# Down product of three of ten row tiles from row-scaled fp16 weight halves, residual added at evacuation

## The reference, cut to what matters

```python
def _ste_round(v):
    return v + jax.lax.stop_gradient(jnp.round(v) - v)
def _act_fake_quant(x, clip_factor):
    scale = sigmoid(clip_factor) * jnp.max(jnp.abs(x)) / QMAX      # one number for the whole tensor
    return jnp.clip(_ste_round(x / scale), -QMAX - 1.0, QMAX) * scale
def _weight_fake_quant(w):
    scale = jnp.max(jnp.abs(w), axis=1, keepdims=True) / QMAX      # one number for each output row
    return jnp.clip(_ste_round(w / scale), -QMAX - 1.0, QMAX) * scale
def ffn(x, clip_x, clip_down, w_gate, w_up, w_down):
    xq = _act_fake_quant(x, clip_x[0])
    gate = jnp.einsum('bsh,ih->bsi', xq, _weight_fake_quant(w_gate))
    up = jnp.einsum('bsh,ih->bsi', xq, _weight_fake_quant(w_up))
    h = _act_fake_quant(jax.nn.silu(gate) * up, clip_down[0])
    return jnp.einsum('bsi,hi->bsh', h, _weight_fake_quant(w_down))
xn = _layernorm(x)
x = x + gcn(xn, edges) + linear_attention(xn)
x = x + ffn(_layernorm(x))
return x
```

## Time and profile before

| what | value |
|---|---|
| median of 3 runs | 743.32 us |
| the profiled execution's own time | 743.04 us |
| its span, first to last instruction | 740.9 us |
| what lies around the span | 2.14 us |
| PE, DVE, POOL, ACT busy | 712.0, 495.0, 272.1, 208.8 us |
| down stage, first matmul to the end | 716.38 to 740.9 us |

### The profile page before, as it was taken

One profiled execution on the slowest core, in us unless ns is written; L12 is line 12 of the kernel. 1 busy time (PEld: TensorE's weight loads), 2 busy tenths in 40 slices (PEclk: granted clock), 3 DMA queues, 4 the chain that ended last, 5 costly groups with the idle time before them and its releaser, 6 DMA issues.

```text
span 740.9 us, 12159 instructions
## 1 busy us (share of the span) xinstructions
PE 712.0 (96%) x3843; PEld 365.9 (49%) x3843; DVE 495.0 (67%) x978; ACT 208.8 (28%) x346; POOL 272.1 (37%) x403
## 2 busy tenths in 40 slices
PE   4999999999999999999999999999999999999993
PEld 2455555555555554566544444444444444445751
DVE  7878887887666656556932213567777778766767
ACT  5133334553333244446212213420000000012440
POOL 4576767898666646540010000011111111110018
PEclk9999999999999999999999999999999999999997
DMA  9752422551000000003030110052222232100506
GB/s 342 216 140 59 108 42 72 171 171 58 0 0 0 0 2 1 2 0 114 1 114 0 67 46 0 23 174 65 57 72 54 61 85 64 33 12 1 114 13 264
DMA packets 52765, 52.20 MB, mean 70 GB/s; under 512 B 36482, under 2 KB 37514, under 8 KB 52720
## 3 DMA queue, kind: packets, MB, share of 16 engines
q1 hardware_dynamic: 52720, 51.61, 23.3%
HBM read 37.96 MB, written 5.12 MB: 58 GB/s over the span
## 4 chain that ended last, share of the span: by engine, by line
PE 69%; issue 12%; DVE 10%; POOL 4%; ACT 2%; DMA 2%; DVEq 1%; POOLq 0%; SPq 0%; ACTq 0%
PE bank L537 31%; PE bank L730 13%; PE bank L703 10%; PE bank L611 10%; POOL mem L496 2%; DVE mem L1032 2%; PE bank L522 2%; ACT mem L830 2%; PE bank L554 2%; DVE counts L1122 2%; DVE mem L1202 1%; DMA mem<-in_x 1%; PE bank L678 1%; DVE mem L1048 1%; DMA mem<-in_L_gnn_W 1%
## 5 line engine op out<-in xcount | busy, mean ns | idle before, releaser
L537 PE MATMUL bank<-mem 128*128 128x512 f16 x1440 | 327.6, 381 | 4.9 <-DVE mem L1048 1.7
L537 PEld LDWEIGHTS bank<-mem 128*128 (+1 forms) x1440 | 137.9, 98 | 158.6 <-issue 7.0
L448 POOL TENSOR_SCALAR hot_src<-iota_p,src_col 125x128 bf16<-125x128 bf16 x252 | 174.5, 707 | 14.1 <-issue 14.1
L1122 DVE TENSOR_TENSOR counts<-bank,counts 128x120 f32 x328 | 92.4, 282 | 49.2 <-issue 8.5
L611 PE MATMUL bank<-mem 128*128 128x512 f16 (+2 forms) x576 | 105.2, 339 | 0.8 <-DVE mem L1161 0.8
L730 PE MATMUL bank<-mem 128*128 128x512 f16 (+1 forms) x504 | 105.5, 369 | 0.0
L703 PE MATMUL bank<-mem 128*128 128x512 f16 x400 | 88.0, 379 | 0.0
L611 PEld LDWEIGHTS bank<-mem 128*128 128x128 f16 (+1 forms) x576 | 55.2, 98 | 42.4 <-DVE mem L1161 1.4
L730 PEld LDWEIGHTS bank<-mem 128*128 128x128 f16 x504 | 49.3, 98 | 53.7
L850 ACT ACTIVATE src_gap<-iota_p,loT 125x128 bf16<-125x128 bf16 x84 | 33.5, 399 | 115.5 <-PE bank L522 106.9
L485 POOL TENSOR_TENSOR mem<-mem 128x1024 f32<-128x1024 f32 x10 | 23.5, 2350 | 113.3 <-DMA mem<-in_L_mix_bo 113.3
(11 more groups left out here) (150 smaller groups left out, 645.7 us busy)
## 6 DMA issues: line engine op xcount, KB each, us to landing
mem<-in_x SPq DMA_DIRECT2D x18, 512.0 KB, 3.9
out_x<-mem SPq DMA_DIRECT2D x9, 512.0 KB
mem<-in_L_mix_Wk SPq DMA_DIRECT2D x4, 1024.0 KB, 9.4
mem<-in_L_mix_Wv SPq DMA_DIRECT2D x4, 1024.0 KB, 8.4
mem<-in_L_mix_Wq SPq DMA_DIRECT2D x4, 1024.0 KB, 5.2
mem<-in_L_gnn_W SPq DMA_DIRECT2D x4, 1024.0 KB, 5.2
mem<-in_L_mix_Wo SPq DMA_DIRECT2D x2, 2048.0 KB, 7.9
mem<-in_L_ffn_w_down SPq DMA_DIRECT2D x4, 352.0 KB, 3.1
```

The source lines that it names most:

```text
L448: pool.tensor_scalar(hot_src[0:EC, i, c, :], iota_p[0:EC, :], src_col[0:EC, i, c:c + 1], None, ALU.is_equal).then_inc(S["hot_src_ready"], 1)
L537: last = pe.matmul(o[:, :], xT[:, a * K + k, bass.ds(t * P, P)], w16[i][:, k, b, :], start=(at == 0), stop=(at == len(parts) - 1))
L1122: dve.tensor_tensor(window, agg[i][:, k * WC:(k + 1) * WC], window, ALU.add).then_inc(S["adj_added"], 1)
```

## The change: what it does

Tiles 3, 6 and 9 (Y_SPLIT) use other weights. Once, POOL multiplies wdT by d_row, scaled by 256 (in tile 9 of stage B, between its L485 and its L487), three instructions of 128x1024; ACT rounds the products to fp16 (the high half), and POOL subtracts the high half from the product (the low half), three more instructions of 128x1024, which wait for q_ready 6. For these tiles TensorE takes 12 matmuls in place of 6, and VectorE's evacuation is result times s_d plus x2, straight into x2: nothing is left to add. The other tiles are evacuated into y_t as before; the addition of tile 8 is VectorE's, whole; those of tiles 0, 1, 2, 4, 5 and 7 are POOL's, whole. wdT and hq are fp16 in place of bf16.

```diff
-Y_DVE = [304] * (T - 1) + [560]
+Y_SPLIT, Y_ON_DVE = (3, 6, 9), 8
+Y_ON_POOL = [t for t in range(T) if t not in Y_SPLIT and t != Y_ON_DVE]
...
+        wd_half = [part(RAW, FB, D, dt=F16), part(C0 + 3 * D, FB, D, dt=F16)]
... SP
+            for t in range(T):
+                rows = LAST if t == T - 1 else P
+                if t in Y_SPLIT:
+                    sp.wait_ge(SC["y_moved"], 2 * t + 2)
+                elif t == Y_ON_DVE:
+                    sp.wait_ge(SC["y_dve"], 1)
+                else:
+                    sp.wait_ge(SC["y_pool"], Y_ON_POOL.index(t) + 1)
+                sp.dma_start(out[P * t:P * t + rows, :], x2[0:rows, t, :]).then_inc(SC["stored"], 16)
... POOL, tile_b, after the addition of the bias
+                if t == T - 1:
+                    pool.wait_ge(SB["agg_full"], 2 * T)
+                    pool.wait_ge(SC["d_row"], 2)
+                    for i in (8, 9):
+                        pool.wait_ge(SF[f"wT_in{i % 2}"], landed[i])
+                    for b, n in enumerate(FR):
+                        pool.tensor_tensor(y_t[b][0:n, :], wdT[0:n, b, :], d_row[0:n, :], ALU.mult).then_inc(SC["wd_scaled"], 1)
                 pool.wait_ge(SB["b_var"], t + 1)
... POOL, after stage B
+            pool.wait_ge(SC["q_ready"], 6)
+            for b, n in enumerate(FR):
+                pool.wait_ge(SC["wd_hi"], b + 1)
+                pool.tensor_tensor(wd_half[1][0:n, b, :], y_t[b][0:n, :], wd_half[0][0:n, b, :],
+                                   ALU.subtract).then_inc(SC["wd_lo"], 1)
-            for t in range(T):
-                s = slice(Y_DVE[t], D)
+            for t in Y_ON_POOL:
...
-                pool.tensor_tensor(x2[:, t, s], x2[:, t, s], y_t[t % 4][:, s], ALU.add).then_inc(SC["y_ready1"], 1)
+                pool.tensor_tensor(x2[:, t, :], x2[:, t, :], y_t[t % 4], ALU.add).then_inc(SC["y_pool"], 1)
... PE, keep_busy
-                    pe.matmul(bank[3][:, :], ident16[:, :], wdT[:, 0, 0:HALF], start=True, stop=True)
+                    pe.matmul(bank[3][:, :], ident16[:, :], wguT[:, 0:2, 0:HALF // 2], start=True, stop=True)
... PE, down stage
+                if t == Y_SPLIT[0]:
+                    pe.wait_ge(SC["wd_lo"], FB)
+                    weights = wd_half if t in Y_SPLIT else [wdT]
                     for b in range(FB):
+                        for w in weights:
+                            last = pe.matmul(y_bank[2 * (t % 4) + n][:, :], hq[0:r, b, t * P:(t + 1) * P],
+                                             w[0:r, b, n * HALF:(n + 1) * HALF], ...)
... ACT, after the weight pieces
+                act.activation(d_row[:, j * HALF:(j + 1) * HALF], kv_acc[j][:, :], ACT.Copy, scale=W_UP).then_inc(SC["d_row"], 1)
+            act.wait_ge(SB["mix_moved"], 2 * T - 2)
+            act.wait_ge(SB["agg_moved"], 2 * T)
+            for b, n in enumerate(FR):
+                act.wait_ge(SC["wd_scaled"], b + 1)
+                act.activation(wd_half[0][0:n, b, :], y_t[b][0:n, :], ACT.Copy).then_inc(SC["wd_hi"], 1)
             act.activation(clip[:, 7:8], clip[:, 6:7], ACT.Silu).then_inc(SC["silu_table"], 1)
... DVE, down stage
-            dve.tensor_tensor(s_d, m_col, clip[:, 5:6], ALU.mult)
+            dve.scalar_tensor_tensor(s_d, m_col, 1.0 / W_UP, clip[:, 5:6], ALU.mult, ALU.mult)
+            dve.wait_ge(SC["wd_lo"], FB)
             for t in range(T):
-                if t >= 4:
-                    dve.wait_ge(SC["y_ready1"], t - 3)
+                if t not in Y_SPLIT and t - 4 in Y_ON_POOL:
+                    dve.wait_ge(SC["y_pool"], Y_ON_POOL.index(t - 4) + 1)
                 for n in range(2):
...
+                    if t in Y_SPLIT:
+                        dve.scalar_tensor_tensor(x2[:, t, half], y_bank[2 * (t % 4) + n][:, :], s_d, x2[:, t, half], ALU.mult,
+                                                 ALU.add).then_inc(SC["y_moved"], 1)
+                    else: ...
-                dve.tensor_tensor(x2[:, t, s], x2[:, t, s], y_t[t % 4][:, s], ALU.add).then_inc(SC["y_ready0"], 1)
+                if t == Y_ON_DVE:
+                    dve.wait_ge(SC["y_moved"], 2 * t + 2)
+                    dve.tensor_tensor(x2[:, t, :], x2[:, t, :], y_t[t % 4], ALU.add).then_inc(SC["y_dve"], 1)
```

More of the change, by code:

```diff
@@ L122, in gps_layer @@
         at += K * FF
-        wdT = part(at, FB, D, dt=BF16)
+        wdT = part(at, FB, D, dt=F16)
         at += FB * D // 2
@@ L138, in gps_layer @@
         hT = part(H0, FB, NP)
-        hq = part(H0 + FB * NP, FB, NP, dt=BF16)
+        hq = part(H0 + FB * NP, FB, NP, dt=F16)
         y_t = [part(H0 + FB * NP * 3 // 2 + i * D, D) for i in range(4)]
         assert FB * NP * 3 // 2 + 4 * D <= T * D
+        wd_half = [part(RAW, FB, D, dt=F16), part(C0 + 3 * D, FB, D, dt=F16)]
         x_half = part(EXTRA, 4, D, dt=F16).rearrange("p (i a) d -> p i a d", a=2)
@@ L160, in gps_layer @@
         raw16 = [part(XT + 2 * SLOT + T * P, D, dt=BF16), hot_dst_mem[:, :]]
+        raw_down = [part(XT + 2 * SLOT + T * P, D, dt=F16), hot_dst_mem[:, :].bitcast(F16)]
         hot_src = sb("hot_src", [P, 2, G, P], BF16)
@@ L198, in gps_layer @@
         SC = sems("clip_in", "c_step", "m_prev", "m_ready", "m_all", "exp", "silu_table", "h_max", "h_rs", "h_8", "hq_first", "d_row", "gus", "xn_columns", "affine", "q_ready", "qT_full",
-                  "qT_moved", "qT_in0", "qT_in1", "qT_in2", "qT_in3", "gate_full", "silu", "up_moved", "h_rounded", "hq", "y_full", "y_moved", "y_ready0", "y_ready1", "stored")
+                  "qT_moved", "qT_in0", "qT_in1", "qT_in2", "qT_in3", "gate_full", "silu", "up_moved", "h_rounded", "hq", "y_full", "y_moved", "y_dve", "y_pool", "wd_scaled", "wd_hi", "wd_lo", "stored")
         def over_tiles(tile):
@@ L376, in transpose_piece @@
                         sp.dma_start_transpose(wdT[:, :, (a + k) * P:(a + k + 1) * P],
-                                               raw16[i % 2][:, k * PITCH:(k + 1) * PITCH]).then_inc(SF[f"wT_in{i % 2}"], 16)
+                                               raw_down[i % 2][:, k * PITCH:(k + 1) * PITCH]).then_inc(SF[f"wT_in{i % 2}"], 16)
             load_piece(0)
@@ L800, in _ @@
                         pe.wait_ge(SC["y_moved"], 2 * t + n - 7)
+                    weights = wd_half if t in Y_SPLIT else [wdT]
                     for b in range(FB):
                         r = FR[b]
-                        last = pe.matmul(y_bank[2 * (t % 4) + n][:, :], hq[0:r, b, t * P:(t + 1) * P],
-                                         wdT[0:r, b, n * HALF:(n + 1) * HALF], start=(b == 0), stop=(b == FB - 1))
+                        for w in weights:
+                            last = pe.matmul(y_bank[2 * (t % 4) + n][:, :], hq[0:r, b, t * P:(t + 1) * P],
+                                             w[0:r, b, n * HALF:(n + 1) * HALF], start=(b == 0 and w is weights[0]),
+                                             stop=(b == FB - 1 and w is weights[-1]))
                     last.then_inc(SC["y_full"], 1)
@@ L934, in piece16 @@
                 if pieces[i][0] == "down":
-                    act.activation(raw16[i % 2][:, 0:2 * PITCH].rearrange("p (k i) -> p k i", i=PITCH)[:, :, 0:FF],
+                    act.activation(raw_down[i % 2][:, 0:2 * PITCH].rearrange("p (k i) -> p k i", i=PITCH)[:, :, 0:FF],
                                    raw8[i % 2][:, 0:2 * FF].rearrange("p (k i) -> p k i", i=FF),
@@ L946, in _ @@
             for j in range(2):
-                act.activation(d_row[:, j * HALF:(j + 1) * HALF], kv_acc[j][:, :], ACT.Copy).then_inc(SC["d_row"], 1)
+                act.activation(d_row[:, j * HALF:(j + 1) * HALF], kv_acc[j][:, :], ACT.Copy, scale=W_UP).then_inc(SC["d_row"], 1)
[4 more added lines that the diff above has]
+                act.activation(wd_half[0][0:n, b, :], y_t[b][0:n, :], ACT.Copy).then_inc(SC["wd_hi"], 1)
             act.activation(clip[:, 7:8], clip[:, 6:7], ACT.Silu).then_inc(SC["silu_table"], 1)
@@ L1432, in _ @@
             dve.tensor_tensor(rs_d, max_inv, clip[:, 7:8], ALU.mult).then_inc(SC["h_rs"], 1)
-            dve.tensor_tensor(s_d, m_col, clip[:, 5:6], ALU.mult)
+            dve.scalar_tensor_tensor(s_d, m_col, 1.0 / W_UP, clip[:, 5:6], ALU.mult, ALU.mult)
             dve.drain()
             dve.tensor_copy(hq[:, :, 0:P], h8[:, :, 0:P]).then_inc(SC["hq_first"], 1)
+            dve.wait_ge(SC["wd_lo"], FB)
             for t in range(T):
-                s = slice(0, Y_DVE[t])
-                if t >= 4:
-                    dve.wait_ge(SC["y_ready1"], t - 3)
+                if t not in Y_SPLIT and t - 4 in Y_ON_POOL:
+                    dve.wait_ge(SC["y_pool"], Y_ON_POOL.index(t - 4) + 1)
                 for n in range(2):
@@ L1443, in _ @@
                     dve.wait_ge(SC["y_full"], 2 * t + n + 1)
-                    dve.scalar_tensor_tensor(y_t[t % 4][:, half], y_bank[2 * (t % 4) + n][:, :], s_d, d_row[:, half], ALU.mult,
-                                             ALU.mult).then_inc(SC["y_moved"], 1)
```

(11 more changed lines are left out.)

## The result

The changed kernel takes 746.02 us (median of 7 runs, 745.03 to 747.12) against 743.50 (7 runs, 743.24 to 744.0): ratio 1.0033, 95% interval 1.0021 to 1.0045. It is slower by 2.5 us, a third of a per cent; 745.9 was forecast. The profiled execution took 745.03, the shortest of the seven, with a span of 743.2 us, so 1.83 us lie around it, where it was 2.14.

What follows compares the result with a forecast made beforehand. It took POOL's additions to bound the kernel's end. Profiled 743.04 plus 4.9 lost in the FFN stage minus 2.3 gained in the down stage gave 745.6, plus 0.28 to the median 745.9 us; range 741.0 to 748.2.

Steps and rivals of the forecast that it cites:

- VectorE's TENSOR_SCALAR and CAST wait for POOL's TENSOR_TENSOR: FFN stage, casts 6 to 9: VectorE's SBUF instructions wait for POOL's running subtraction to end; for CAST this was assumed.
- The term of 4.9 us: FFN stage: POOL's three subtractions after the sixth cast delay VectorE, so TensorE's unit 3 and everything behind come 4.9 us later.
- the likeliest case: The forecast itself: loss 4.1 to 5.3 us, gain 1.4 to 3.2, total 744.4 to 747.2; chance 0.57.
- The bound of 4.1: FFN stage: the loss is 4.1 us if VectorE gets two instructions in between two of POOL's.
- TensorE has no cover: FFN stage: TensorE already waits for up(1) and up(3), so VectorE's delay passes on in full, 4.9 us.
- The down stage, 2.3 us: Last stage: with split tiles and tile 8 added by VectorE, the last store is issued earlier; gain 2.3 us.
- Nothing in stage B: POOL's multiplications end at 673.7, 4.2 us before tile 9's power; with ACT's roundings they cost nothing.
- What lies around the span: Time of the execution outside the profiled span: 2.14 us, carried into the sum as it was.
- rival 3: FFN stage: POOL keeps its turn, loss 6.3 us, and TensorE's clock falls; 747.3 to 749 us; chance 0.12.
- Rivals 1: FFN stage: VectorE is not held, or TensorE has cover; faster, 741.1 us; chance 0.17.
- 2: FFN stage: only TENSOR_SCALAR is held, not CAST; loss 2.9 us, total 743.9, no change that can be told; chance 0.13.
- 4: Stage B: POOL's multiplications end too late for tile 9's power, needing 3.75 us each or a start 4.2 late; rest, 0.01.

Runs made afterwards that it cites:

- experiment 3: Changed kernel with POOL's subtractions waiting for the ninth cast instead of the sixth, leaving one CAST beside them: 742.32 us, ratio 0.9988 to the kernel before.
- Experiment 4: Changed kernel with 13 dummy matmuls in TensorE's stop before unit 3: 745.00 and 745.06 us; the changed kernel unchanged, timed again: 745.63 us.
- experiment 5: Changed kernel with subtractions after the tenth cast and VectorE's addition of tile 8 moved behind tile 9's first half: 741.17 us, ratio 0.9970 to the kernel before.
- experiment 1: Changed kernel with POOL's three subtractions waiting for the tenth cast instead of the sixth: 740.69 us against 743.33 for the kernel before, ratio 0.9970.
- experiment 2: Kernel before plus only POOL's three subtractions after the sixth cast, result unused, with VectorE's down stage waiting for them: 747.64 us, ratio 1.0065.
- experiment 8: Kernel before with SP's store loop written out as ten stores with fixed addresses: 743.08 us, ratio 0.9995.
- experiment 6: Changed kernel with subtractions after the tenth cast and no split tiles, VectorE adding tiles 3, 6, 8 and 9 whole: 744.15 us, ratio 1.0011 to the kernel before.

## Why the prediction was right

The mechanism, its place and its sign were right, and both large terms are in the profile. That the total agrees within 0.1 us is luck, since errors cancelled. For the profiled execution the working gave 745.6, and 745.03 came, 0.6 less. From there to the median it allowed 0.28 us, and it is 0.99.

- *VectorE's TENSOR_SCALAR and CAST wait for POOL's TENSOR_TENSOR.* Right, in the order foretold: TENSOR_SCALAR 6, cast 6, cast 7, and none behind. The unknown, CAST, was decided by experiment 3. The rule cited from the Trainium skill ("SBUF — State Buffer", Who interferes with whom) agrees with the trace for both: 1.99 us in place of 0.80 and of 0.69.
- *The term of 4.9 us* was mis-sized: 4.07. The row of 1024 columns with two f32 inputs (2.35 us) stood for the subtractions; with one 16-bit input they take 2.13. Three times 0.22 are 0.66 of the 0.83 too much. The rest is in how a turn passes on: each held instruction ends 0.54 or 0.55 us after POOL's record does (691.74 after 691.20, 694.26 after 693.72, 696.80 after 696.25), where the working had 0.66 to 0.69. The result lies just below the likeliest case's own bounds (4.1 to 5.3). The bound of 4.1 was for another course, two VectorE instructions between two of POOL's, which did not happen. Medians of one chip put the place at 4.5 us (745.63 - 741.17, experiments 4 and 5), and at 4.3 with the stop filled (745.00 - 740.69, experiments 4 and 1).
- *TensorE has no cover.* Right: it stopped for up(1), up(2) and up(3), and nothing was made good behind.
- *The down stage, 2.3 us.* Right, 2.31 to the last store; the addition of tile 8 took 2.12 us as foretold (2.1). The 0.2 us allowed for the stores' backlog was left out of the sum and is 0.4.
- *Nothing in stage B.* Right: POOL done at 673.2, with 4.9 us to spare.
- *What lies around the span* was taken as unchanged and is 0.31 less.
- *The clock* was in rival 3 and is real in part of the executions. Experiment 4 makes it part of why the median (+2.52) lies above the profiled execution (+1.99). Rival 3's other half, POOL keeping its turn, did not happen.
- *Rivals 1, 2 and 4* are out: VectorE was held, CAST too, and the multiplications were early.

The experiments also give the version to keep: the change with the subtractions after the tenth cast, 740.69 us, 0.3% faster than the kernel before; the change as made is 0.3% slower than it (0.9970 against 1.0033).

## What to carry to other kernels

Before giving POOL an idle-looking stretch, list which of VectorE's instructions stand there: if it is TENSOR_SCALAR or CAST between SBUF tensors, each may wait for the whole POOL instruction, and here 6.4 us of POOL work that nobody waited for cost 4.1 us of the end. Beside evacuations from PSUM and reductions the same work cost nothing. Look at a stage's last store as well as its last instruction: of 2.31 us gained on the engines 1.90 came to the end, while the last stores stood in a queue.

## What was not expected of the hardware

- A POOL TENSOR_TENSOR of 1024 columns takes 2.12 to 2.15 us with one f32 and one 16-bit input, either way round (L496 writes f32, L506 fp16), and 2.35 with two f32 (L489).
- After the same stop of TensorE, 3.36 to 3.37 us, the granted clock stayed full in one profiled execution of the changed kernel and fell to half in another, and in experiment 2, for about 3.5 us.
- The kernels with the change have 1.74 to 1.87 us around their span, those without 2.08 to 2.19, whatever their length. It is not the store loop (experiment 8), nor the use of the split tiles (experiment 6: 1.83). The cause stays open.
